# Attention: several narrow diagonal units of the row maximum share one PSUM bank

## The reference

```python
x = x + 0.5 * ffn(layernorm(x));  x = x + attn(layernorm(x));  x = x + 0.5 * ffn(layernorm(x))
# attn, per head:
scores = where(causal, -inf, q @ k.T / sqrt(D))
out = softmax(scores) @ v            # softmax subtracts each row's maximum
```

## Time and profile before

| | us |
|---|---|
| median of 3 runs | 1399.8 |
| lowest and highest | 1398.54, 1399.95 |
| the profiled execution, its own time | 1402.6 |
| its span, first to last instruction | 1400.8 |
| mean granted TensorE clock | 0.96 of full |

### The profile page before, as it was taken

One profiled execution on the slowest core, in us unless ns is written; L12 is line 12 of the kernel. 1 busy time (PEld: TensorE's weight loads), 2 busy tenths in 40 slices (PEclk: granted clock), 3 DMA queues, 4 the chain that ended last, 5 costly groups with the idle time before them and its releaser, 6 DMA issues.

```text
span 1400.8 us, 22187 instructions
## 1 busy us (share of the span) xinstructions
PE 1284.7 (92%) x8224; PEld 779.2 (56%) x8224; DVE 1145.8 (82%) x2638; ACT 858.5 (61%) x1157; POOL 227.2 (16%) x205
## 2 busy tenths in 40 slices
PE   4999999966799999999999999999999989999996
PEld 3888888844444444444444444444444435888886
DVE  6578888887689899999999899989999953677875
ACT  4655555511067676776777677767766777656654
POOL 4003222342220020110110110200101021001000
PEclk9999999966679999999999999999999999999999
DMA  3124444863165080260440710800701131344312
GB/s 114 52 68 143 143 143 128 170 208 99 46 120 71 2 130 10 35 97 10 70 63 10 109 24 10 124 16 17 116 9 37 50 91 47 83 132 138 93 46 75
DMA packets 88740, 110.30 MB, mean 79 GB/s; under 512 B 25308, under 2 KB 60892, under 8 KB 87004
## 3 DMA queue, kind: packets, MB, share of 16 engines
q1 hardware_dynamic: 88632, 108.88, 33.5%
HBM read 64.62 MB, written 42.21 MB: 76 GB/s over the span
## 4 chain that ended last, share of the span: by engine, by line
PE 70%; DVE 20%; ACT 6%; issue 3%; DMA 0%; DVEq 0%; POOL 0%; ACTq 0%; SPq 0%
PE m_ps L1092 19%; PE o_ps L1129 17%; DVE maxes L1029 9%; PE s_ps L1113 6%; PE ups_a L610 6%; PE yps_c L627 5%; PE yps_a L627 5%; PE ups_c L610 4%; PE gps_a L658 4%; DVE masked L1032 3%; ACT probs L1008 3%; DVE xmv_a L392 2%; PE gps_c L643 2%; PE tps_a L636 1%; PE gps_a L643 1%
## 5 line engine op out<-in xcount | busy, mean ns | idle before, releaser
L1008 ACT ACTIVATE probs<-s_ps 128x1024 f32<-128x1024 f32 (+3 forms) x640 | 538.9, 897 | 224.0 <-PE s_ps L1113 223.1
L1029 DVE TENSOR_REDUCE maxes<-m_ps 128x1 f32<-128x512 f32 x768 | 489.4, 683 | 46.4 <-PE m_ps L1092 45.1
L1092 PE MATMUL m_ps<-kT,qT 64*128 64x512 f32 (+3 forms) x1280 | 453.5, 456 | 42.5 <-DVE maxes L1029 17.1
L1092 PEld LDWEIGHTS m_ps<-kT,qT 64*128 64x128 f32 x1280 | 205.2, 188 | 387.3 <-DVE maxes L1029 261.4
L1113 PE MATMUL s_ps<-qT,kT 64*128 64x512 f32 (+3 forms) x1280 | 309.9, 393 | 6.9 <-ACT probs L1008 6.5
L1129 PE MATMUL o_ps<-probs,v_w 128*32 128x512 f32 (+3 forms) x2560 | 306.2, 551 | 0.6 <-POOL probs L977 0.2
L1032 DVE CUSTOM_DVE_ANT_0 masked<-m_ps,mask 128x128 f32<-128x128 f32 (+3 forms) x512 | 235.8, 486 | 44.3 <-PE m_ps L1092 38.8
L977 POOL TENSOR_SCALAR_AFFINE_SELECT probs<-probs 128x512 f32<-128x512 f32 x128 | 82.2, 642 | 674.1 <-ACT probs L1008 674.1
L1113 PEld LDWEIGHTS s_ps<-qT,kT 64*128 64x128 f32 x1280 | 167.3, 189 | 31.6 <-ACT probs L1008 29.3
L1129 PEld LDWEIGHTS o_ps<-probs,v_w 128*32 128x32 f32 x2560 | 50.8, 108 | 73.3 <-issue 56.8
L506 DVE TENSOR_TENSOR h_lo_c<-hsq_c,h_hi_c 128x512 fp32r<-128x512 f32 x64 | 46.1, 722 | 53.3 <-ACT h_hi_c L343 28.9
(11 more groups left out here) (124 smaller groups left out, 1889.1 us busy)
## 6 DMA issues: line engine op xcount, KB each, us to landing
qT<-qkT_parts SPq DMA_DIRECT2D x96, 128.0 KB
kT<-qkT_parts SPq DMA_DIRECT2D x48, 256.0 KB
qkT_parts<-qk_hi_a SPq DMA_DIRECT2D x32, 256.0 KB, 4.6
qkT_parts<-qk_lo_a SPq DMA_DIRECT2D x32, 256.0 KB, 4.8
sumsT<-osum SPq DMA_DIRECT2D x32, 256.0 KB, 2.4
table_a<-in_rot SPq DMA_DIRECT2D x8, 768.0 KB, 7.7
xin_a<-in_x SPq DMA_DIRECT2D x8, 512.0 KB, 3.6
xres_a<-in_x SPq DMA_DIRECT2D x8, 512.0 KB, 5.0
```

The source lines that it names most:

```text
L1008: act.activation(probs[:, b % PBUF, 2 * hp:2 * hp + 2, off:CH], s_ps[hp][:, :, off:CH], ACT.Exp, scale=D ** -0.5).then_inc(exp_done, 1)
L1029: dve.tensor_reduce(out, m_ps[:, i % MB, 0:width], AX.X, ALU.max).then_inc(max_read, 1)
L1092: pe.matmul(m_ps[:, i % MB, 0:width], qT[n % 2][r0:r0 + HR, j, hp, t * P:(t + 1) * P], kT[n % 2][r0:r0 + HR, hp, k * CH:k * CH + width], s ...
```

## The change

A unit becomes an item that may hold two parts in one bank. On the diagonal, the widths 128 and 384 of one head go together (128 + 384 columns), two heads' 256 go together, and 512 stays alone. Both parts have the same `par`. TensorE waits once, writes both parts and signals once, with the second; VectorE waits once, reduces both, and signals once. The matmuls and reduces are the same in number and size as before. `place_units` now puts one diagonal item second in each slot, as long as there are any, and plain ones elsewhere. A group has 136 items and 4 turns, where it had 160 units and 4 turns.

```diff
+UNITS = []
+for j in range(NJ):
+    for k in range(j):
+        UNITS += [(j, par, [(t, hp, k, CH, 0)]) for t in range(T) for hp in range(G // 2) for par in range(2)]
+    UNITS += [(j, par, [(0, hp, j, P, 0), (2, hp, j, 3 * P, P)]) for hp in range(G // 2) for par in range(2)]
+    UNITS += [(j, par, [(1, hp, j, 2 * P, 2 * P * hp) for hp in range(G // 2)]) for par in range(2)]
+    UNITS += [(j, par, [(3, hp, j, CH, 0)]) for hp in range(G // 2) for par in range(2)]
...
-    cost = [u[5] + 110 for u in UNITS]
+    cost = [sum(width + 110 for _, _, _, width, _ in parts) for _, _, parts in UNITS]
...
-    def fit(u, behind):
-        return (UNITS[u][5] <= CH // 2) != behind, UNITS[u][3] == par
+    def fit(u, own):
+        j, up, parts = UNITS[u]
+        return (parts[0][2] == j) != own, up == par
...
-            u = min(rest, key=lambda u: fit(u, len(slots[g]) == T - 1))
+            u = min(rest, key=lambda u: fit(u, len(slots[g]) == 1))
...
             dve.wait_ge(max_done, i + 1)
-            out = maxes[:, j % 2, par, hp, t, k:k + 1]
-            if k < j:
...
+            for t, hp, k, width, at in parts:
+                out = maxes[:, j % 2, par, hp, t, k:k + 1]
+                if k < j:
+                    last = dve.tensor_reduce(out, m_ps[:, i % MB, 0:width], AX.X, ALU.max)
+                else:
+
+                    last = dve.tensor_tensor_reduce(masked[:, i % MB, at:at + width], m_ps[:, i % MB, at:at + width],
+                                                    mask[:, CH - width:CH], 1.0, NEG, ALU.add, ALU.max, out)
+            last.then_inc(max_read, 1)
...
             free_bank(e)
             r0 = HR * par
-            pe.matmul(m_ps[:, i % MB, 0:width], qT[n % 2][r0:r0 + HR, j, hp, t * P:(t + 1) * P],
-                      kT[n % 2][r0:r0 + HR, hp, k * CH:k * CH + width], start=True, stop=True).then_inc(max_done, 1)
+            for t, hp, k, width, at in parts:
+                last = pe.matmul(m_ps[:, i % MB, at:at + width], qT[n % 2][r0:r0 + HR, j, hp, t * P:(t + 1) * P],
+                                 kT[n % 2][r0:r0 + HR, hp, k * CH:k * CH + width], start=True, stop=True)
+            last.then_inc(max_done, 1)
```

More of the change, by code:

```diff
@@ L747, in step_no @@
     return NJ * n + j
-UNITS = [(j, t, hp, par, k, CH if k < j else P * (t + 1))
-         for j in range(NJ) for t in range(T) for hp in range(G // 2) for k in range(j + 1) for par in range(2)]
+UNITS = []
[5 more added lines that the diff above has]
+    UNITS += [(j, par, [(3, hp, j, CH, 0)]) for hp in range(G // 2) for par in range(2)]
 def place_units():
@@ L778, in place_units @@
             slots[g].append(u)
-            done, par = done + cost[u], UNITS[u][3]
+            done, par = done + cost[u], UNITS[u][1]
     assert not any(left)
@@ L1019, in unit @@
         def unit(e):
-            j, t, hp, par, k, width = UNITS[e[2]]
+            j, par, parts = UNITS[e[2]]
             i = ITEM[e]
```

## The result

The changed kernel takes 1386.74 us, the median of 4 runs (1385.59 to 1390.94), where the kernel before took 1399.88 beside it on the same chip. The ratio is 0.9897, with a 95% interval of 0.9871 to 0.9923. The forecast was 1400.6, with a range from 1391 and "no change" as the likeliest. The kernel is 1% faster, and the forecast missed by 13.9 us.

A forecast was written before the change was run, and what follows sets the result against it. Waiting between TensorE and VectorE through the ring of three banks was taken as what the change can move. Attention +6.5 us and first stage -5.7 gave +0.8 us, put onto the median as 1400.6, range 1391 to 1410.

The forecast's parts named there:

- the loop: Attention, exactly four items between two products: three banks close a loop through the first item behind them, 2.70 us per interval.
- Interval 18's sum: Attention, full items alone: products 1.00, to VectorE's start 0.53, read 0.76, to the next products 0.42, sum 2.71 us.
- the first stage: First group's units among the feed-forward projections: TensorE waits for fewer bank reads ahead of them, together -5.7 us.
- POOL's rotation: First feed-forward stage: if this or the stores bind in place of the banks, all but about 1 us is lost.
- kind 2: Attention, four items, a double one first (22, 30): fill about 0.1 longer, reads 0.10 more; 2.92 us each, 5.84 per group.
- kind 5: Attention, three items between products: TensorE writes 0.2 us longer where the last or middle is double; 22.2 per group.
- the turns: Attention intervals 5 and 25 at 3.25 us, with 0.22 less to read ahead, and 32 at 2.92; together 9.4 per group.
- kind 3: Attention, four items, shorter products: 2.47 us three times, 4.88 for 13 and 14, 2.35 each for 6 and 26; together 17.0.
- rival E: Attention: second parts wait for a whole weight load, 0.18 us in ten places per group; 13.5 on top, 1414; chance 0.07.
- the clock: Granted clock 0.96 over the span; a few lower-level stretches more or fewer in the attention would hide the whole difference.
- C: Faster: first stage gives 5.7 us, attention even if three-item intervals stand 0.1 lower and turns wait less; 1394.1; chance 0.23.
- B: Slower: the loop of three banks costs the attention 6.5 us, the first stage gives nothing back; 1406.3; chance 0.27.

The follow-up runs named there:

- old_first: The changed kernel, but the first group's units one to a bank and in the old order; 1395.38 us, ratio 0.9957.
- before_set: The kernel before, but GpSimd's second memset of kT waits until VectorE has the first norm's scale; 1400.41 us, ratio 0.9986.
- before_hold: The kernel before, but both GpSimd memsets of kT start only after VectorE's reciprocal of the norm; 1404.47 us, ratio 1.0015.
- short_read: The changed kernel, but VectorE reduces only 128 of 512 columns of a plain item first behind the products; 1344.44 us, ratio 0.9583.
- even room: Slot room 2.5 for 1 in `place_units`: on the changed kernel 1356.06 us, ratio 0.9663; on the kernel before 1386.02, ratio 0.9912.
- room10: The changed kernel with 10 for 1 in each slot's room (14, 13, 12, 11); 1369.69 us, ratio 0.9763.

## Why the prediction was wrong

**Right: the loop.** Interval 18's sum of 2.71 held wherever it applied, the shortened read moved these intervals and left the four-item ones with a masked item first, and five banks showed it one cadence longer.

**Right: the first stage,** -5.7 for -6.1 (-5.4 to -6.1 over three traces of either order, `old_first` left aside), moved alone by one experiment and left alone by the other. The steps are right only in the rough: I had put all of it on fewer bank reads, and half stayed when each part had its own bank; and that single steps come out within 0.6 us is in part luck, since the clock moves them by 1. That POOL's rotation might bind in place of the banks didn't happen.

**Wrong: the price of a second part (kinds 2 and 5).** I read "0.23 behind the first" off as a fixed cost of a matmul on the same rows half. But those are matmuls of 512 columns, and 0.23 is about what each streams. The trace shows 0.11 behind 256 columns and 0.06 to 0.07 behind 128. The parts of a double item have 512 columns together, no more than one full unit. So TensorE writes both in about the time of a single item: of the 0.2 that I put on each of six three-item intervals, [13] costs nothing (28) and [22] 0.08 (33), and the 0.1 on 22 and 30 wasn't there. No row of mine shows two short matmuls of one rows half behind each other, and I should have looked for some. This is most of the net 1.5 us per group: kind 5 stands 0.9 below its sum, although interval 9 is 0.13 above its own, and kind 2 0.25. The rest is interval 4, whose products I took for full ones (0.2), and the turns (0.2); kind 3 came out 0.16 longer. Over 7.5 groups that is 11.5 us of the 13.9. Interval 21, with its two values, makes this uncertain by some 0.2 a group.

The page's rule, rival E, fell further. Here the second part's load is recorded with 0.19 us from 640.64, while the first part runs on the same rows half, and TensorE starts the second part 0.07 behind the first and has all three matmuls done within 0.47. The Trainium skill, "TensorE: Matmul & The Clock Gate", Part 3, "The mechanism", lets a weight load overlap matmuls in flight only when the row group differs, though it also has loads into a background weight buffer pulled ahead; the trace contradicts the first and fits the second.

**Wrong: the clock left aside.** The attention gained 7.1 us, of which the order is 0.67 x 7.5 = 5.0. The other 2.1 fit the stretches at the lower clock, 34.9 us in before's attention and 29.9 in after's. With the old order, `before_set` had 24.7 and took 781.3, `before_hold` 38.4 and took 786.2. Before, three fell into the attention's first seven groups, in the intervals behind a turn. The windows of before around one (us, busy of PE, PEld, DVE, ACT, POOL with instructions, PEclk, DMA share, GB/s):

```profile
448.00:452.00 4.00, 3.33 (x28) 1.53 (x27) 3.81 (x11) 2.68 (x4) 0.00 (x0) 1.00 0.01 3
452.00:459.00 7.00, 6.99 (x33) 3.32 (x33) 5.35 (x15) 4.63 (x6) 0.00 (x0) 0.51 0.11 39
459.00:463.00 4.00, 4.00 (x30) 1.52 (x22) 3.06 (x12) 2.57 (x3) 0.00 (x0) 1.00 0.00 0
```

The granted clock is 1.00, then 0.51 for 7 us (1.2 GHz in place of 2.4), then 1.00 again. TensorE had been busy for 3.33 of the 4.00 us before. A stretch of 3.4 us makes a group of the old order 1.2 to 1.5 longer (98.25 for 96.85). After had one in its first seven groups, at 969.3, and a longer one in the last group, where there are no units. Over the fourteen traces, sixteen such stretches begin in the attention's first seven groups at the end of interval 5 or 25 or within 1.5 us of the start of 6 or 26, so behind a turn each time; one other, in `short_read`, begins in the wait of 4 us for the keys. With even room, in either kernel, none fell behind the first group (5 and 25 take 2.65 to 2.96 there, 3.45 to 3.48 in before), but neither did one with each part in its own bank, where they take 3.09. So the stretches follow the turn's wait, but its length alone doesn't say when one comes, and they fall into different groups in kernels of the same order. I had named the clock as what could hide my difference, and gave it no chance.

**Of the rivals,** C was nearest: the first stage's 5.7 and "three-item intervals stand 0.1 below my sums and the turns wait less". They stood up to 0.3 below. B's mechanism is real, 0.4 to 0.8 per interval of four items whose first went from narrow to full or double (4: 2.12 to 2.49, 35: 2.14 to 2.70, 22: 1.97 to 2.79), but it had been counted in the sum already and the rest outweighed it. **The range** failed by adding its ends up too mildly: -8 for the attention "at the very outside" and -5.7 make 1386.1, and I had cut that corner off at 1391.

Interval 9 takes 2.63 since TensorE isn't the bound in it: its second scores wait for ScalarE's exponential, which my sum for three items left out:

```profile
592.49 3.35 ACT L1015 ACTIVATE probs<-s_ps 128x1024 f32<-128x1024 f32 x4 [1.03 <-PE s_ps L1124]
...
594.48 0.19 PEld L1124 LDWEIGHTS s_ps<-qT,kT 64*128 64x128 f32 x2 [0.62 <-ACT probs L1015]
```

Open: why interval 21 takes 2.23 in some groups and 2.67 in others, and why a stretch of the lower clock follows one turn and not the next.

## What to carry to other kernels

In a ring of banks, count the items between two long pieces of work of the engine that fills them: once there is one more than banks, the item right behind the long piece sets the loop, and its read counts in full, whatever the average of busy times says. Ask first whether the items could be spread so that fewer intervals close the loop at all: that gave, on top of the shared banks, twice what these had. The price of one more small matmul is read from a pair of its own size: here the start-to-start time grew with the columns of the first one. And a range has to reach the sum of the ends of its terms wherever these may err in the same direction.

## What the runs showed of the hardware

- A second matmul in the same rows half starts 0.06 to 0.07 us behind one of 128 columns, 0.11 behind one of 256 (both in after) and 0.23 behind one of 512. Its own weight load, recorded with 0.18 to 0.19, is hidden in all three.
- A VectorE `tensor_scalar` on 128x4 elements in SBUF takes 0.17 us, but if a GpSimd memset is under way it waits it out: 3.55 in before and 3.23 in `before_hold`, ending within 0.05 of the memset's end. `tensor_tensor` isn't held: L462 took 2.29 beside the memset. The Trainium skill, "SBUF — State Buffer", "Who interferes with whom", says that a VectorE operation in a 2-port mode and GpSimd share a port pair, that `tensor_scalar` can enter such a mode, and that the later one blocks fully; the trace agrees in who is held and for how long, while the mode itself shows in no row.
- Between the latest start of L383 that the second memset let through (11.98, `room10`) and the earliest that it held (12.01, `short_read`) lie 0.03 us. The first matmul starts at 14.20 in the one and at 17.64 in the other, with the same instructions up to there: two profiles are to be compared from a common point on.
